# Attention in two halves of the token blocks, with the expert mixture of blocks 0 and 1 issued block by block beside the attention of blocks 2 and 3

## The reference

```
x = norm(x + A(x))        # energy = x^T x (256x256), softmax, mix
x = norm(x + B(x))        # 8 experts' LoRA on a gated MLP of 896, top 2
x = norm(x + C(x))        # causal attention, 16 heads of 16
x = norm(x + D(x))        # 32 experts of inner width 96, top 8 with a share rule

C: q, k, v = x Wqkv; probs = softmax(causal(q k^T / 4)); out = (probs v) Wo^T
D: combine = routed weights [2048, 32];  out = sum_e combine_e * (silu(x Wg_e) * (x Wu_e)) Wd_e
```

## Time and profile before

| | |
|---|---|
| median of 3 runs | 1611.99 us |
| the three runs | 1615.75, 1611.99, 1581.69 us |
| profiled execution | 1600.74 us |
| its span, first to last instruction | 1599.0 us |
| mean granted clock of TensorE | 0.91 |
| TensorE busy | 1464.6 us (92%) |
| VectorE busy | 936.7 us (59%) |
| ScalarE busy | 627.5 us (39%) |
| GpSimd busy | 262.4 us (16%) |

### The profile page before, as it was taken

One profiled execution on the slowest core, in us unless ns is written; L12 is line 12 of the kernel. 1 busy time (PEld: TensorE's weight loads), 2 busy tenths in 40 slices (PEclk: granted clock), 3 DMA queues, 4 the chain that ended last, 5 costly groups with the idle time before them and its releaser, 6 DMA issues.

```text
span 1599.0 us, 20300 instructions
## 1 busy us (share of the span) xinstructions
PE 1464.6 (92%) x7956; PEld 1043.3 (65%) x7956; DVE 936.7 (59%) x1777; ACT 627.5 (39%) x884; POOL 262.4 (16%) x343
## 2 busy tenths in 40 slices
PE   6689999999999889999999999888889999999995
PEld 5578778788788655344443443454478888888885
DVE  3555753754745457678758878763345545575445
ACT  3032322422322212466546656545523444444331
POOL 3220110200200001012111211301011222232221
PEclk9699999999999865699869999977889999999998
DMA  6000000000000438002400600000001111111110
GB/s 267 0 1 1 1 1 1 0 1 1 20 1 27 149 119 117 1 2 35 46 2 5 77 2 1 21 10 1 1 21 40 45 45 50 50 41 50 50 57 27
DMA packets 31831, 55.41 MB, mean 35 GB/s; under 512 B 6392, under 2 KB 13304, under 8 KB 31224
## 3 DMA queue, kind: packets, MB, share of 16 engines
q1 hardware_dynamic: 29688, 53.85, 13.6%
q0 software_dynamic: 2048, 0.27, 0.2%
HBM read 43.21 MB, written 10.49 MB: 34 GB/s over the span
## 4 chain that ended last, share of the span: by engine, by line
PE 79%; DVE 14%; ACT 4%; issue 3%; POOL 0%; DMA 0%; POOLq 0%; DVEq 0%; ACTq 0%
PE ps L1449 50%; PE ps L1647 9%; PE ps L1717 9%; PE ps L1695 4%; DVE mpart L1236 4%; PE ps L1666 1%; DVE x L1039 1%; PE ps L1471 1%; PE ps L1456 1%; PE ps L1502 1%; ACT probs L940 1%; PE ps L1487 1%; PE ps L1726 1%; PE ps L1513 1%; DVE mpart L1246 1%
## 5 line engine op out<-in xcount | busy, mean ns | idle before, releaser
L940 ACT ACTIVATE probs<-ps 128x1024 f32<-128x1024 f32 (+3 forms) x320 | 277.6, 896 | 238.2 <-PE ps L1695 237.2
L1449 PE MATMUL ps<-xtd,gu 128*128 128x512 f32 x1152 | 283.5, 401 | 7.8 <-DVE x L1279 4.8
L1236 DVE TENSOR_REDUCE mpart<-ps 128x1 f32<-128x512 f32 x384 | 238.0, 682 | 49.8 <-PE ps L1647 49.6
L1647 PE MATMUL ps<-stack 48*128 48x512 f32 (+3 forms) x832 | 232.9, 425 | 36.3 <-DVE mpart L1236 21.0
L1449 PEld LDWEIGHTS ps<-xtd,gu 128*128 128x128 f32 x1152 | 216.3, 191 | 58.8 <-issue 9.8
L1647 PEld LDWEIGHTS ps<-stack 48*128 48x128 f32 x832 | 129.2, 213 | 180.4 <-DVE mpart L1236 110.2
L1449 PE MATMUL ps<-ma,b 128*128 128x512 f32 x672 | 169.0, 401 | 10.3 <-DVE x2f L1185 7.4
L1695 PE MATMUL ps<-stack 50*128 50x512 f32 (+3 forms) x640 | 171.0, 449 | 5.5 <-ACT probs L940 5.4
L1717 PE MATMUL ps<-probs,vaug 128*32 128x512 f32 (+3 forms) x1280 | 172.8, 617 | 1.9 <-POOL probs L820 1.6
L1449 PEld LDWEIGHTS ps<-ma,b 128*128 128x128 f32 x672 | 126.9, 191 | 44.1 <-DVE x2f L1185 10.7
L1449 PEld LDWEIGHTS ps<-dn,hpart 128*128 128x128 f32 x1152 | 144.3, 189 | 5.3 <-DVE hpart L1020 1.0
(11 more groups left out here) (175 smaller groups left out, 1676.9 us busy)
## 6 DMA issues: line engine op xcount, KB each, us to landing
gu_raw<-in_wgu SPq DMA_DIRECT2D x48, 256.0 KB, 2.6
stack<-qk_dram SPq DMA_DIRECT2D x72, 128.0 KB, 9.1
qk_dram<-qk_out SPq DMA_DIRECT2D x16, 512.0 KB, 2.9
dn_raw<-in_wdn SPq DMA_DIRECT2D x48, 128.0 KB, 2.7
stack<-qk_dram SPq DMA_DIRECT2D x48, 64.0 KB, 2.4
x<-in_x_tm SPq DMA_DIRECT2D x4, 512.0 KB, 5.1
xt_in<-in_x_fm SPq DMA_DIRECT2D x1, 2048.0 KB, 8.4
out<-x SPq DMA_DIRECT2D x4, 512.0 KB, 3.1
```

The lines of the kernel that those rows point to most:

```text
L940: act.activation(probs[:, (2 * r + p) % 4, :, off:BLK], banks(bank)[:, :, off:BLK], ACT.Exp, scale=float(HD) ** -0.5).then_inc(exp_done.se ...
L1236: ins = dve.tensor_reduce(part[:, p, qt % TPB, 2 + kb:3 + kb], ps[:, bank, :], AX_X, ALU.max)
L1449: mm = pe.matmul(out, lhs(i), rhs(k), start=first and n == 1, stop=last and n == todo, **more)
L1647: return pe.matmul(out, stack[lo:lo + KROWS, g % 2, 0, b, p, P * t:P * (t + 1)], stack[lo:lo + KROWS, g % 2, 1, kb, p, k0:k0 + width], sta ...
```

## The change

The order of the work is now written out as a string, `ORDER` (1411 letters), one letter for an entry, and `attention_plan` only reads it.
- The rounds are reordered into eight visits: groups 0 to 3 with query blocks 0 and 1, and then groups 0 to 3 with blocks 2 and 3. `stack` becomes `keys0`, `keys1`, `queries0`, `queries1`; a visit loads its keys (2 or 4 blocks) and its 2 blocks of queries (`load_visit`).
- Blocks 0 and 1 so have all their groups after 48 of the 160 steps. Their `turnO` to `ce` lie in the first two visits of the second half.
- Their stage D is 48 passes of one block instead of 24 of two. A pass is now five entries: `gate` (6 matmuls, G), `up` (6, U), `split` (i), `low` (l), `down` (12, D). 42 of the 48 lie among units and steps of blocks 2 and 3, six behind the last step, among the output and router of block 3. Blocks 2 and 3 keep 24 passes of two blocks.
- Weights are loaded and split in 72 passes instead of 48. SyncE now walks the plan too.
- Gate and up share bank 7, each one bank wide, so units, `max` and `out` have banks 4 and 5 from the first gate on. From the first down on banks 2 and 3 hold the sums of stage D, and scores and wide entries have the pair 0-1 alone.
- ScalarE's copy for `ce` 0 and the head's output have one wait more each, on events long past.

```
-    steps = [(g, qb, kt) for g in range(NG) for qb in range(NB) for kt in range(TPB * (qb + 1))]
-    rounds = [(g, qb) for g in range(NG) for qb in range(NB)]
+    visits = [(half, g) for half in range(2) for g in range(NG)]
+    rounds = [(g, 2 * half + i) for half, g in visits for i in range(2)]
+    steps = [(g, qb, kt) for g, qb in rounds for kt in range(TPB * (qb + 1))]
...
+    wide, single = [0, 2], [4, 5, 7]
...
+        elif letter == "D":
+            if n == 0:
+                wide, taken["pair"] = wide[:1], 0
+            plan.append(("down", n, 2))
...
+            if letter == "G" and n == 0:
+                single, taken["one"] = single[:2], 0
+            kind, key = chain[letter], n + 1 if letter in "TX" else n
+            bank = pair() if letter in "VTabdex" else 7 if letter in "GU" else None
...
+            def gate_alone(n, bank):
+                pe.wait_ge(*wd_lo.after(n))
+                if n % JT == 0:
+                    pe.wait_ge(*d_lo.after(n // JT))
+                bank_free(pe, "gate", n)
+                gate_or_up(n, 0, bank).then_inc(gate_ps.sem, 1)
+
+            def down_alone(n, bank):
+                pe.wait_ge(*h_part_lo.after(n))
...
+            def hidden_alone(n, bank):
+                dve.wait_ge(*gated.after(n))
+                dve.wait_ge(*up_ps.after(n))
+                if n:
+                    dve.wait_ge(*h_part_lo.after(n - 1))
+                dve.tensor_tensor(hmul1[:, :], ps[:, bank, :], silu1[:, :], ALU.mult).then_inc(h_mul.sem, 1)
+                dve.wait_ge(*h_mul.after(n))
...
+                elif kind == "whi" and key + 3 < len(passes):
+                    sp_.wait_ge(*wd_lo.after(key))
+                    raw_weights(key + 3)
```

More of the change, by code:

```diff
@@ L68, in attention_plan @@
[L68 to L157, removed]
@@ L290, in attention_plan @@
-    assert not todo and not at_step, (len(todo), at_step)
-    end = len(rounds) - 1
-    while to_head:
-        head()
-    move = [i for i, e in enumerate(plan) if e[:2] in (("pv", len(steps) - 1), ("ucopy", end), ("out", end), ("head", end))]
-    kept = {plan[i][0]: plan[i] for i in move}
-    for i in reversed(move):
-        del plan[i]
-    if ("out", end) not in [e[:2] for e in kept.values()]:
-        kept["out"] = ("out", end, ones[count["one"] % 3])
-    pair("gu", (0, 0, 0), 2)
-    mark("pv", len(steps) - 1)
@@ L345, in attention_plan @@
-    mark("down", (1, JT - 1))
-    mark("acc", 1)
-    return steps, rounds, units, closes, plan
+        units += [("diag", g, qb, i, a) for i in range(2) for a in range(2)] + [("half", g, qb, 0, a) for a in range(2)]
+        units += [("part", g, qb, p, a) for p in range(HP) for a in range(2)]
+        units += [("full", g, qt, kb, p, a) for qt in range(TPB * qb, TPB * (qb + 1)) for kb in range(qb) for p in range(HP)
+                  for a in range(2)]
+        closes[units[-1]] = n
+    ends = {max(i for i, s in enumerate(steps) if s[:2] == gq): n for n, gq in enumerate(rounds)}
@@ new lines, in attention_plan @@
+    bm = [(b, m) for b in range(NB) for m in range(2)]
+    chain = {"a": "turnO", "b": "proj", "c": "normC", "d": "turnD", "e": "logit", "r": "rexp", "s": "best", "f": "share",
+             "k": "kept", "m": "combine", "x": "ce", "V": "v", "T": "turnC", "G": "gate", "U": "up", "i": "split", "l": "low",
+             "A": "acc", "n": "statD", "z": "normD", "w": "whi", "X": "load"}
+    once = {"L": "lora", "R": "resB", "N": "normB", "W": "raws", "y": "wo", "Y": "wg1"}
+    plan, count, taken, turned, left = [], collections.Counter(), collections.Counter(), [], []
@@ L350, in build @@
+    plan.append(("down2", JT - 1, None))
+    return rounds, steps, units, closes, plan
 def build(nc, x_tm, x_fm, w13_d, a13_d, b13_d, w2a2_d, b2_d, wg0_d, wqkv_d, wo_d, wg1_d, wgu_d, wdn_d,
@@ L507, in build @@
         mix_read = sig("mix_read", range(NT))
-        blocks = [(st, b) for st in "ABCD" for b in range(NB)]
+        rounds, steps, units, closes, plan = attention_plan()
+        blocks = [(st, b) for st in "AB" for b in range(NB)]
+        blocks += [({"resC": "C", "statD": "D"}[kind], key) for kind, key, bank in plan if kind in ("resC", "statD")]
+        blocks += [("D", b) for b in range(2, NB)]
         var_ready = sig("var_ready", blocks)
@@ L633, in build @@
                 held_by[6] = (kind, key)
-            elif bank is not None:
-                mine = range(bank, bank + (1 if kind in ("unit", "max", "out") else 2))
+            elif bank is not None and (kind != "down" or key % JT == 0):
+                mine = range(bank, bank + width.get(kind, 2))
                 before[kind, key] = sorted({held_by[b] for b in mine}, key=str)
-                held_by.update({b: (kind, key) for b in mine})
+                held_by.update({b: (kind, key // JT if kind == "down" else key) for b in mine})
         def bank_free(eng, kind, key):
@@ L740, in _ @@
+            for b in range(2, NB):
+                store(b)
             sp_.wait_ge(stored, 16 * NB)
```

610 lines of the change are left out of this document (290 added, 320 removed).

## The result

The change made the kernel slower: 1619.42 us in the median of four runs (1613.51 to 1624.89) against 1598.84 us for the kernel before (1581.69 to 1615.75). The ratio is 1.0191, with a 95% interval from 1.0104 to 1.0278. Some executions of a kernel run slower at a lower granted clock, and the ratios leave these out, so 1.0191 is not the quotient of the two medians. Forecast was 1565 us, 2 to 3% faster. The profiled execution of after took 1624.89 us, with a span of 1623.2.

A forecast was written before the change was run, and what follows sets the result against it. TensorE was taken as the full engine, losing time to idle gaps and low clock. First gate 937 + mixed stretch 407 + pair stage 203 + end 16 = 1563, plus 1.7 outside the span, 1565 us; range 1512 to 1630, eight in ten.

The forecast's parts named there:

- the price of the single score pair: Mixed stretch: scores waiting for their one bank pair, bounded by 0 and 43 us over 144 scores, taken near 0.
- ScalarE: 144 x 0.896 + 42 x 2.3 = 226 us: ScalarE's work for 144 scores and 42 passes in about 360 us, used to call TensorE the full engine.
- Neither ring decides by its sum: Mixed stretch: score pair 216 us and shared gate/up bank 176 us, each of 360; order could still make either decide.
- The ledger: TensorE busy time times clock: first gate to pair stage holds 395 us of content, density rising from 0.85 to 0.97.
- "ScalarE's idle time" as the cover of the splits: Mixed stretch: 24 additional weight splits, ScalarE 25 and GpSimd 48 us, hidden by idle time of both engines.
- The check that I named: TensorE's weight-load idle on exponentials in the mixed stretch: under 15 us expected; 40 or more would blame the single score pair.
- Bank 7: Gate and up sharing one bank in the mixed stretch: 4.2 us a pass, 176 of 360 us, not deciding by sum.
- The first gate at 937: End of the first stretch: 900 - 9 for fewer units + 32 outputs and router + 16 short rounds = 939, say 937.
- my second rival: First half: short rounds fall to half clock, costing 25 to 40 us, total 1590 to 1605, no change; chance 0.20.
- SyncE's queue: Last visit's load stands behind a `wd_lo` wait, its keys needed some 40 steps later; costed at nothing, 10 us if late.
- The one on the slow side: Mixed stretch: few banks make TensorE pause and its clock fall; density 0.80, 494 us, total 1652; chance 0.14.
- the 407 of the forecast: Length from first gate to start of the pair stage: 395 us of content at density 0.97 gives 407 us.

The follow-up runs named there:

- the copy version: Kernel after with the 48 single-block passes' silu replaced by a plain copy, changing what layer D computes for blocks 0 and 1: 1575.37 us, ratio to before 0.9809.
- the last run: Kernel after with a tanh gate, its VectorE product at the up's place, up in banks 4 and 5, and early key loads for visits 2 and 3: 1568.09 us.
- the run with three banks: Kernel after, silu kept, with gate and up taking banks 4, 5 and 7 in turn with the units: 1615.40 us, ratio to before 1.0082.
- keys ahead: Kernel after with the keys of visits 2 and 3 loaded early into unused blocks of the key tiles: 1599.32 us, ratio to before 0.9996.
- the late gate: Kernel after with tanh for silu, its VectorE product moved to the up's place, and up in banks 4 and 5: 1595.24 us, ratio to before 0.9975.
- the tanh version: Kernel after with the single-block gate made as g * (1 + tanh(g/2)), product at the gate's place, bank 7 kept: 1634.38 us, ratio to before 1.0174.
- the run without the interleaving: Kernel after with all 48 single-block passes moved behind the last value product, two score pairs and three maxima banks kept through attention: 1773.46 us, ratio to before 1.1088.

## Why the prediction was wrong

**The step that failed** is the price of the single score pair, "Bounds: 0, and 0.3 us for each of 144 scores, 43 us. I take near 0", and under it the sentence "ScalarE: 144 x 0.896 + 42 x 2.3 = 226 us" with what it was used for, "Neither ring decides by its sum". I took the functions' durations from stretches where only one of them runs, and laid them side by side. For these the sum was right: from 936 to 1353 ScalarE is busy for 309 us, and without the loads for 217. But between them come 72 loads of 1.283 us, 92 us of ScalarE that the sum put at nothing, and they stand before the exponential that frees the only score pair. A turn of the ring was put at 1.5 us "with handoffs"; the one shown took 3.5, with 1.48 us of idle TensorE in it. Taking the loads away gave 41 of the 64 us, 35 of them among the units. The row was there to read, since the trace of before has the same instruction wherever silu and exponential meet, 12 in all, too few to stand on the page.

Point by point:
- *The ledger.* Content after the first gate 411 us against 395, so 16 us too low; density 0.87 against 0.97. The idea, that content stays and density moves, held: in the eleven traces that have it the mixed part holds 407 to 415 us of content, and its length goes from 431 to 619 us. Its density by this reckoning is 0.88 in after (413 of 471 us), 0.66 with more loads, 0.95 in the copy version and 0.93 in the last run.
- *"ScalarE's idle time" as the cover of the splits.* In the copy version TensorE's waits for exponentials are down to 9.4 us with all 24 more splits in place. That cover holds.
- *The bounds on the score pair, 0 to 43 us.* The loads cost 41, near the upper end, by a cause that I had not seen. The check that I named, a wait on `probs` of 40 us or more, came out at 40.8 us, and would have blamed the single pair alone. With the pair single and no loads the wait is 9.4 us, so the loads make the delay. That a second pair would have covered them is likely, and no run has it.
- *Bank 7.* Put at no cost; 7 to 12 us by the run with three banks, and 20 where tanh and its product hold the bank.
- *The first gate at 937.* It came at 935.8, and that is luck, from terms that were wrong and cancelled. The waits for loads of visits, put at nothing, were 26 us. The clock of the short rounds was 0.66 from 612 to 778, which was my second rival. Against them, the scores began at 564 instead of 614, which I had also put at nothing. The keys ahead bring the first gate 34 us forward against after in one trace and, with the late gate, 18 against its own; the load term by itself is not known better than that.
- *SyncE's queue.* I asked what stands behind `wd_lo` in the mixed stretch, where nothing was late, and not what 24 issues are to a visit that is a third as long.
- *The rivals.* The one on the slow side had the right place, the ring of few banks, and its mechanism is a part of what happened: TensorE's clock is 0.95 and 0.96 in the mixed stretch, and of the 471 us of the mixed part 36 are idle and 22 lost to the clock (435 us busy, 413 of content). In the copy version it is 14 and 8. The rule of the Trainium skill on bank cycling (TensorE: Matmul & The Clock Gate, "A second HAM failure mode: psum-queue depth-cycling") was not borne out as a matter of the cycling alone: the copy version and the last run cycle the same single score pair, and their clock in the mixed part is 0.98 and 0.99. With 84 more loads and the same banks it is 0.84.
- *The rule that I should have weighed* is in the Trainium skill, ScalarE: Activation LUTs, "Table sets: the hidden batching unit": functions of one set need no load between them, those of different sets do, and tanh is in the set of exp. The trace agrees on both counts. The figure that the Trainium skill gives on the same page under "What ACT_TABLE_LOAD costs", about 2.66 us for a switch, load and drain, is not what stands here: silu ends at 1126.07, the load starts at 1126.09, and the exponential at 1127.38, 1.3 us in all.

What stays open: between the copy version's 431 us and the 407 of the forecast are 24 us, about 14 of them content (409 us against 395) and the rest density. I did not separate the turn of the score pair, the change between 128-row and 48-row weights, and the router of block 3 in the last six passes.

## What to carry to other kernels

When two stages are laid side by side, add up for each engine not only the durations but what changes between them: the list of functions on ScalarE above all, since a load of 1.28 us appears only where they alternate. Its price is that of its place: 0.1 us here where TensorE is full, 0.8 where units, scores and one pair of banks wait on each other, and more than its duration where ScalarE has nothing left to give. An instruction that waits in an in-order queue costs all that stands behind it; the same instruction moved to where its input is ready was worth 33 to 38 us here. To find out whom it delays, cut the stretch where the kind of work changes: my explanation by the maxima did not survive that. And when work is cut into shorter pieces, compare the time to refill a buffer with the new length of a piece.

## What was not expected of the hardware

- A load takes 1.283 us each time, for exponential, silu and back; tanh between exponentials needed none (75 loads in after at the exponentials of the steps and the gates of the single passes, one in the tanh version).
- With dense 128-row products between attention's small ones the granted clock of the mixed part is 0.94 to 0.99, and 0.84 with 84 more loads; attention by itself, in the run without the interleaving, ran its last 235 us at 0.56 with TensorE busy for 85% of them.
- Twelve DMA issues in ScalarE's order per visit took back what they gave: TensorE's waits for loads fell by 23 us and those for exponentials rose by 27 (570 to 950), although ScalarE was busy for 39% of 612 to 778. The kernel's ratio to before is 1.031, that of after 1.0191, with intervals that overlap.
